# Unread products of two constant tiles in TensorE's waits: the last dense layer and the output stage of a graph network

## The chip, the cores and the metric

The kernel runs as one program on one core of a Trainium2 chip. The metric is device time in microseconds (us), from one launch, as the median of several runs. The engines are named as in the profile: PE is TensorE (PEld its weight loads), DVE is VectorE, ACT is ScalarE, POOL is GpSimd, SP is SyncE, which issues most DMAs here.

## The reference

The reference is a graph network of four blocks on 12,500 nodes with 128 features each and 212,500 edges sorted by destination. Each block normalizes x, computes a message-passing layer and adds its result to x:

```python
h = jnp.maximum(_layernorm(x, axis=-1), 0.0)
x = x + _L2_gnn_ref(h, edge_index, ...)      # ends with a batch norm and h @ fcW.T + fcb
h = jnp.maximum(_layernorm(x, axis=-1), 0.0)
x = x + _L3_gnn_ref(h, edge_attr_20, edge_weight, src, dst, ...)
# inside _L3_gnn_ref:
h = x @ W_in2f
Wij = ssp(f_ij @ W_filt1 + b_filt1) @ W_filt2 + b_filt2
Wij = Wij * rcut_ij[:, None]
x_ij = h[idx_j] * Wij
agg = jax.ops.segment_sum(x_ij, idx_i, num_segments=n_atoms)
out = ssp(agg @ W_out1 + b_out1) @ W_out2 + b_out2
```

`ssp` is the softplus less log 2. The first two blocks (relational layers with ten and three relations) and the third (two mean-aggregating layers) have the same form: a dense product per node, then a sum over edges.

## The kernel before, in words

Nodes are taken in 25 superblocks of 512 (four tiles of 128), edges in 104 groups of 16 tiles of 128. The kernel has seven edge passes, with dense stages (the list `DENSE`, k = 0 to 6) between them. A dense stage turns the sums of the pass before into the new x, normalizes it, and writes a table of products that the next pass gathers by edge. Stages 2, 3 and 4 ("flows") run mostly inside the pass that follows their data: `flow_keep` (L1741, all three stages) and `flow_init` (L1750, stages 3 and 4) are VectorE's parts of it, once for each of 25 superblocks. They stand between the one-hots and additions of the edge groups on VectorE's queue.

The change touches these functions, and the dense stages k = 5 and k = 6, which run by themselves, with no edge work beside them. Every engine has its own instruction stream; the order within one is the order in which the code is written, and engines meet at semaphores (`wait_ge`, `then_inc`).

**Stage 5, the last layer's dense work**, is a loop over superblocks with `body(f, l)` where f is one ahead of l. On TensorE a turn is: wait for y_ready; `update(f)` (L1561, L1562: for each of four tiles a product of one row of ones with the bias row fcb, then yT by fcw, into bank 0); wait for h; four transposes of h (L1592, bank 1); wait for hT; four products with the table's weights (L1604, banks 3 to 6). VectorE adds the update to xs (L2120), takes the layer norm's statistics (L2127 to L2137) and evacuates half of the table products (L2146). ScalarE makes, in this order, yT from the batch norm (L1179), hT (L1191), the square root (L1195), h (L1205) and the other half of the evacuations (L1213). SP stores x (L709) and loads the next xs (L705), POOL stores the table (L869).

**The filter pass**, the last edge pass, follows. Its `filter_product` opens with L1412, the product of `ones_b` (96 rows by 128, bf16) with `bfilt2_quad` (96 by 512, bf16), which spreads a bias over a bank. Both tiles are constant from the start of the kernel on.

**Stage 6, the output stage**, runs the same loop over superblocks in pairs. On TensorE a turn is: wait for the four partial sums of superblock f to be added (VectorE L2106, agg_step); four transposes (L1571, bank 1); wait for y_sum of the superblock before; `update(l)` with bout2 and wout2 (L1561, L1562); wait for y_copy and out_parts; one product of 512 columns, wout1 by the copied sums (L1580, bank 7). ScalarE copies the transposes (L1183) and makes the softplus in four steps (L929 to L934); VectorE adds the partial sums (L2106), the two softplus terms (L2111) and the update to xs (L2120). SP issues, in this order, four loads of partial sums for two superblocks ahead (L699), the load of xs (L705), and the store of x (L709); each is 256 KB.

PSUM banks 7 (in stage 5) and 5 (in stage 6) are not in use in their stages.

Of the kernel before, what the change touches and what calls it, by code (L numbers as in the profile page):

```python
# [68 lines left out]
def build(nc, d, out, n_nodes, n_edges):  # L69
# [9 lines left out]
    def turns(k, flag):  # L79

        return nsb * sum(bool(flag(p)) for j, p in enumerate(DENSE[:k]) if j and j not in FLOWS)
# [4 lines left out]
    def has_upd(p): return p["upd"] != ""  # L86
    def has_ln(p): return p["ln"]
    def has_root(p): return p["root"] != ""
    def has_table(p): return p["rels"] > 0
# [5 lines left out]
    def n_chunks(p):  # L95

        return 4 * len(cuts(p))
# [10 lines left out]
    def units(reps):  # L108

        return reps * in_pass + (nsb - in_pass)  # L110

    def stages_with(k, flag):

        return sum(bool(flag(DENSE[j])) for j in FLOWS if j < k)
# [19 lines left out]
    with ExitStack() as ctx:  # L134
        def sb(name, shape, dt=F32):
            return ctx.enter_context(nc.sbuf_tensor(name, shape, dt))

        def sem(name):
            return ctx.enter_context(nc.semaphore(name))
# [42 lines left out]
        bfilt2_quad = sb("bfilt2_quad", [3 * PART, BANK], BF16)  # L182
        bias_rest = sb("bias_rest", [1, P])
        part_b = sb("part_b", [1, P], BF16)
        ones_b = sb("ones_b", [3 * PART, P], BF16)
# [84 lines left out]
        ps = [ctx.enter_context(nc.psum_tensor(f"ps{k}", [P, BANK], F32)) for k in range(8)]  # L270
# [113 lines left out]
        s_keep = sem("s_keep")  # L384
        s_init = sem("s_init")
# [27 lines left out]
        def reps_of(e):  # L413

            e.wait_ge(reps_ready, 1)
            return e.value_load(reps_i[0:1, 0:1], min_val=1, max_val=nwin)

        def settle(e):

            e.sem_inc(settled, 1)  # L420

        def quads_before(reps, pn):

            return reps * (pn * 4 * ngroups)
# [41 lines left out]
        def tail(e, reps, body):  # L466

            with e.Fori(0, nsb - in_pass) as i:
                body(i + in_pass, e.snap(reps * in_pass + i))

        def so_far(reps, k, flag, t):

            return units(reps) * stages_with(k, flag) + t

        def chunks_so_far(reps, k, t):

            return units(reps) * flow_chunks(k) + t * n_chunks(DENSE[k])

        def all_chunks(reps, k):

            return units(reps) * flow_chunks(k + 1)
# [765 lines left out]
        def _(pe):  # L1247
# [13 lines left out]
            reps = reps_of(pe)  # L1261
# [204 lines left out]
            for c in range(n_attr):  # L1466
                n = min(P, ntiles - c * P)
                if c >= 4:
                    pe.wait_ge(typeT_ready, c - 3)
                pe.matmul(ps[c % 4][0:n, 0:P], etype[:, c * P:c * P + n], ident[:],  # L1470
                          start=True, stop=True).then_inc(typeT_mm, 1)
# [62 lines left out]
            for k, p in enumerate(DENSE):  # L1534
                if k == 0:
                    continue
                nck = n_chunks(p)
                hT = hT_s if has_ln(p) else yT
                pe.wait_ge(add_done, quads_before(reps, k + 1) + 4)
                settle(pe)  # L1540
                if k in FLOWS:
                    t = pe.snap(reps * in_pass)
                    pe.wait_ge(c_evac, chunks_so_far(reps, k, t) + 4)
                    if has_root(p):
                        pe.wait_ge(s_init, so_far(reps, k, has_root, t) + 1)
                    settle(pe)
                    tail(pe, reps, lambda f, t: flow_tail(k, f, t))
                    pe.wait_ge(c_evac, all_chunks(reps, k) + 4)
                    pe.wait_ge(s_init, units(reps) * stages_with(k + 1, has_root) + 1)
                    pe.wait_ge(s_x_new, units(reps) * stages_with(k + 1, has_x) + 1)  # L1550
                    settle(pe)
                    run_pass(k + 1)
                    continue

                def update(i):

                    pe.wait_ge(x_new, i + (turns(k, has_x) + 1))
                    for j in range(4):
                        o = ps[0][:, j * P:(j + 1) * P]
                        if "row" in p:  # L1560
                            pe.matmul(o, ones[0:1, :], bias_row[p["row"]][:], start=True, stop=False)  # L1561
                        mm = pe.matmul(o, yT[:, j * P:(j + 1) * P], W[p["upd"]][:], start="row" not in p, stop=True)  # L1562
                    mm.then_inc(upd_mm, 1)

                def body(f, l, b=0, uses=0):
                    if p["src"] == "sum":
                        if f is not None:
                            pe.wait_ge(agg_step, f * 3 + 3)
                            pe.wait_ge(y_copy, f + 1)
                            for j in range(4):  # L1570
                                mm = pe.matmul(ps[1][:, j * P:(j + 1) * P], agg_in[:, b, 0, j, :], ident[:],  # L1571
                                               start=True, stop=True)
                            mm.then_inc(aggT_mm, 1)
                        if l is not None:
                            pe.wait_ge(y_sum, l + 2)
                            update(l)
                        if f is not None:
                            pe.wait_ge(y_copy, f + 2)
                            pe.wait_ge(out_parts, f + 1)
                            pe.matmul(ps[7][:], W["wout1"][:], flat(h), start=True, stop=True).then_inc(out_mm, 1)  # L1580
                        return
                    if f is not None and has_upd(p):
                        pe.wait_ge(y_ready, f + (turns(k, has_src) + 1))
                        update(f)
                    if l is None:
                        return
                    if has_ln(p):
                        n = turns(k, has_ln)
                        pe.wait_ge(h_ready, l + (n + 1))
                        pe.wait_ge(hT_ready, l + (n + 1))  # L1590
                        for j in range(4):
                            mm = pe.matmul(ps[1][:, j * P:(j + 1) * P], h[:, j, :], ident[:], start=True, stop=True)  # L1592
                        mm.then_inc(hT_mm, 1)
                        pe.wait_ge(hT_ready, l + (n + 2))
                    elif has_table(p):
                        pe.wait_ge(y_ready, l + (turns(k, has_src) + 1))
                    if has_root(p):
                        pe.wait_ge(acc_init, l + (turns(k, has_root) + 1))
                        pe.matmul(ps[2][:], W[p["root"]][:], hT[:], start=True, stop=True).then_inc(root_mm, 1)
                    for c in range(nck):  # L1600
                        j, cut = c // len(cuts(p)), cuts(p)[c % len(cuts(p))]

                        pe.wait_ge((evac_a, evac_v)[c % 2], l * (nck // 2) + (chunks(k) // 2 + c // 2 + 1))
                        pe.matmul(ps[3 + c % 4][:, 0:cut[1] - cut[0]], hT[:, j * P:(j + 1) * P],  # L1604
                                  W[p["table"]][:, cut[0]:cut[1]], start=True, stop=True).then_inc(tab_mm, 1)

                superblocks(pe, p, body)
                if has_table(p):

                    pe.wait_ge(evac_a, 2 + chunks(k + 1) // 2)  # L1610
                    pe.wait_ge(evac_v, 2 + chunks(k + 1) // 2)
                    pe.wait_ge(acc_init, turns(k + 1, has_root) + 1)
                    pe.wait_ge(x_new, turns(k + 1, has_x) + 1)
                    run_pass(k + 1)
# [3 lines left out]
        def _(dve):  # L1618
# [62 lines left out]
            reps = reps_of(dve)  # L1681
# [53 lines left out]
            def flow_keep(k, f, t, adds):  # L1735

                acc_f = acc[:, bass.ds(f * SB, SB)]
                dve.wait_ge(add_done, adds)
                dve.wait_ge(s_y, so_far(reps, k, has_src, t) + 2)
                settle(dve)  # L1740
                dve.tensor_scalar(acc_f, acc_f, keep, bias_once, ALU.mult, ALU.add).then_inc(s_keep, 1)  # L1741

            def flow_init(k, f, t, bank, adds):

                acc_f = acc[:, bass.ds(f * SB, SB)]
                dve.wait_ge(add_done, adds)
                dve.wait_ge(s_root, so_far(reps, k, has_root, t) + 2)
                dve.wait_ge(s_keep, so_far(reps, k, has_src, t) + 2)
                settle(dve)
                dve.scalar_tensor_tensor(out=acc_f, in0=ps[bank][:], scalar=once, in1=acc_f, op0=ALU.mult, op1=ALU.add  # L1750
                                         ).then_inc(s_init, 1)

            def flow_x(k, t):

# [466 lines left out]
```

## Time and profile before

| what | value |
|---|---|
| median of three runs | 17679.55 us (17678.54 to 17693.12) |
| the profiled execution | 17666.72 us, its span 17665.0 us |
| mean granted TensorE clock | 0.623 |
| PE / PEld busy | 7873.9 us (45%) / 6273.0 us (36%) |
| DVE busy | 6843.6 us (39%) |
| ACT busy | 3221.2 us (18%) |
| POOL busy | 10730.4 us (61%) |
| mean DMA traffic | 81 GB/s |

The page is read from the top: busy time of each engine, then the course over 40 slices, then the chain of work that ended last. A granted clock of 1.0 is 2.4 GHz and one of 0.5 is 1.2 GHz; a number between them is a mean over a stretch in which both were granted. A share of busy time is a mean over stages with different limits, so the stages are read one at a time, by stretches of the span.

### The profile page before, as it was taken

What the parts mean: (1) busy time and instruction counts of PE and PEld (TensorE: products, weight loads), DVE (VectorE), ACT (ScalarE), POOL (GpSimd) and SP (SyncE); (2) the same over time, 40 slices, a digit from 0 to 9 for tenths busy, and PEclk for the clock granted to TensorE, in tenths of its full rate; (3) what the DMA queues carried; (4) which work ended last, traced back from release to release, by engine and by line L of the source; (5) the groups of instructions that cost most, each with busy time, mean ns of one, the idle gap of its engine ahead of it and who ended that gap; (6) DMA issues with size and microseconds to landing.
All of it is one profiled execution on the core that took longest, in us unless ns stands there. A gap on an engine that the chain in (4) does not pass through costs nothing.

```text
span 17665.0 us, 179568 instructions
## 1 busy us (share of the span) xinstructions
PE 7873.9 (45%) x36107; PEld 6273.0 (36%) x36108; DVE 6843.6 (39%) x28057; ACT 3221.2 (18%) x6961; POOL 10730.4 (61%) x10236
## 2 busy tenths in 40 slices
PE   5633333623333333333333333333333577777777
PEld 3333333322222223332332322222222455555555
DVE  8522222244444423323322222344544344444443
ACT  3422222300000000000000000000000144444443
POOL 0266666365555546666566666666666268888882
PEclk8755555856666555555555555555555577777775
DMA  2333333411111131111111111233333266666665
GB/s 102 125 88 89 89 88 88 175 47 53 54 54 53 53 104 53 52 52 51 51 46 46 47 47 47 60 87 85 87 86 87 66 113 118 117 117 118 117 118 122
DMA packets 1122539, 1438.17 MB, mean 81 GB/s; under 512 B 211981, under 2 KB 737444, under 8 KB 1122316
## 3 DMA queue, kind: packets, MB, share of 16 engines
q0 software_dynamic: 536912, 792.85, 21.0%
q1 hardware_dynamic: 531700, 613.30, 11.9%
q10 hardware_dynamic: 53748, 30.36, 0.6%
q14 instruction: 155, 1.27, 0.0%
q8 instruction: 24, 0.39, 0.0%
HBM read 1101.27 MB, written 334.40 MB: 81 GB/s over the span
## 4 chain that ended last, share of the span: by engine, by line
another core or an unknown queue 29%; issue 22%; DVE 21%; DMA 10%; POOL 6%; PE 5%; ACT 3%; DVEq 2%; ACTq 1%; SPq 0%; POOLq 0%
DMA agg_dram<-acc,sum_row 9%; DVE tab_s L1950 5%; POOL agg_dram L887 5%; DVE scratch L1950 4%; DVE xn_h L1958 3%; DVE scratch L1920 3%; DVE acc L1906 2%; DVE rows L1818 1%; PE ps L1604 1%; POOL scratch L901 1%; ACT hT_s L1009 1%; PE ps L1361 1%; PE ps L1561 1%; PE ps L1562 1%
## 5 line engine op out<-in xcount | busy, mean ns | idle before, releaser
L901 POOL DMA_INDIRECT scratch<-table_dram,row_st x4160 | 3966.4, 953 | 2541.5 <-ACT row_st L1040 1269.3
L901 POOL DMA_INDIRECT rows<-table_dram,row_st x4160 | 3964.0, 953 | 2321.5 <-issue 1247.3
L1361 PE MATMUL ps<-tab_s,rows 128*128 128x128 f32 x8320 | 1906.8, 390 | 3028.0 <-issue 1274.0
L1361 PE MATMUL ps<-scratch 128*128 128x128 f32 x8320 | 1829.5, 390 | 2873.1 <-DMA scratch<-table_dram,row_st 1247.8
L887 POOL DMA_INDIRECT agg_dram<-acc,sum_row x1664 | 2654.5, 1595 | 529.2 <-issue 391.2
L1361 PEld LDWEIGHTS ps<-tab_s,rows 128*128 128x128 f32 x8320 | 1694.4, 294 | 3214.8 <-issue 2149.0
L1361 PEld LDWEIGHTS ps<-scratch 128*128 128x128 f32 x8320 | 1617.8, 289 | 3058.3 <-issue 2119.2
L1906 DVE TENSOR_TENSOR acc<-ps,acc 128x128 f32 x2080 | 608.6, 293 | 4575.8 <-remote 4054.7
L1950 DVE TENSOR_SCALAR scratch<-ps,rw_st 128x128 f32<-128x128 f32 x3328 | 1114.3, 401 | 338.4 <-issue 227.4
L1920 DVE SCALAR_TENSOR_TENSOR scratch<-iota,rw_st,ps 128x128 f32<-128x128 f32 x2496 | 715.2, 343 | 1355.3 <-remote 873.9
L1950 DVE TENSOR_SCALAR tab_s<-ps,rw_st 128x128 f32<-128x128 f32 x3328 | 1112.2, 401 | 330.3 <-issue 247.0
L1271 PE MATMUL ps<-scratch,tab_s 128*128 128x128 f32 x3328 | 675.9, 367 | 808.0 <-DVE scratch L2041 774.6
L1040 ACT ACTIVATE row_st<-row_i 128x16 int32 (+1 forms) x520 | 109.3, 210 | 4819.1 <-remote 3200.6
L1271 PEld LDWEIGHTS ps<-scratch,tab_s 128*128 128x128 f32 x3328 | 595.9, 269 | 866.7 <-issue 866.1
L2035 DVE COPY sum_row<-etype 128x4 int32 x416 | 81.8, 197 | 1476.0 <-POOLq L886 1421.2
L1958 DVE SCALAR_TENSOR_TENSOR xn_h<-scratch,src_st,lower 128x128 f32<-128x128 int32 x1664 | 508.5, 347 | 346.8 <-issue 346.7
L1450 PE MATMUL ps<-scratch,acc 128*128 128x128 f32 x3328 | 601.1, 341 | 12.2 <-issue 7.3
L1450 PEld LDWEIGHTS ps<-scratch,acc 128*128 128x128 f32 x3328 | 566.0, 256 | 20.2 <-issue 20.1
L1406 PE MATMUL ps<-scratch,wfilt 20*128 20x512 f32 x836 | 557.5, 751 | 28.6 <-DMA scratch<-in_feat 22.3
L1414 PEld LDWEIGHTS ps<-wfilt,scratch 128*128 128x128 f32 x3336 | 516.7, 221 | 16.2
L1414 PE MATMUL ps<-wfilt,scratch 128*128 128x128 f32 x3336 | 513.6, 305 | 0.0
L946 ACT ACTIVATE yT<-acc 128x512 f32 (+1 forms) x75 | 47.2, 629 | 2352.9 <-DVE acc L1906 2330.7
(229 smaller groups left out, 10600.9 us busy)
## 6 DMA issues: line engine op xcount, KB each, us to landing
scratch<-in_src_row SPq DMA_DIRECT2D x832, 256.0 KB
table_dram<-tab_s POOLq DMA_DIRECT2D x200, 640.0 KB, 3.2
scratch<-type_dram SPq DMA_DIRECT2D x416, 256.0 KB
scratch<-in_dst_row SPq DMA_DIRECT2D x416, 256.0 KB
rows<-table_dram,row_st POOLq DMA_INDIRECT x4160
scratch<-table_dram,row_st POOLq DMA_INDIRECT x4160
scratch<-table_dram SPq DMA_DIRECT2D x416, 64.0 KB
agg_dram<-acc,sum_row POOLq DMA_INDIRECT x1664
```

What stands on the lines that cost most here:

```text
L887: pool.indirect_dma_start(agg_dram[j], bass.IndirectOffsetOnAxis(ap=sum_row[:, QUAD * q + j:QUAD * q + j + 1], axis=0), sums[:, q, j * P:( ...
L901: pool.indirect_dma_start(row_banks[bank][:, u, :], None, table_dram[k], bass.IndirectOffsetOnAxis(ap=row_st[:, bank, u:u + 1], axis=0)).t ...
L1009: act.activation(hT_s[:], type_row[:, q % 2, :], ACT.Abs, bias=rel_of[:, 3:4]).then_inc(relT_step, 1)
L1271: mm = pe.matmul(o, lhs[:, u, :], rhs[:, u, :], start=j == 0 or not summed, stop=j == QUAD - 1 or not summed)
L1361: mm = pe.matmul(ps[bank][:, q * P:(q + 1) * P], rows[:, u, :], hot[:, u, :], start=u % QUAD == 0, stop=u % QUAD == QUAD - 1)
L1406: pe.matmul(ps[4][:], wfilt1[:], feat[:, q, :], start=True, stop=True).then_inc(f1_mm, 1)
L1414: mm = pe.matmul(ps[6 + b][:, j * P:(j + 1) * P], f_buf[:, 2, b, j * P:(j + 1) * P], W["wfilt2"][:], start=False, stop=j == QUAD - 1)
L1450: mm = pe.matmul(ps[5][:, j * P:(j + 1) * P], hotT[:, q % 2, j * P:(j + 1) * P], nodes[:, q % 2, :], start=True, stop=True)
L1906: dve.tensor_tensor(window, ps[bank][:, q * P:(q + 1) * P], window, ALU.add).then_inc(add_done, 1)
L1920: i = dve.scalar_tensor_tensor(out=out(u), in0=iota[:], scalar=rw[:, 0, u:u + 1], in1=looked_up(j), op0=ALU.is_equal, op1=ALU.mult, accum_ ...
L1950: one_hots(q, lambda u: dve.tensor_scalar(hot[:, u, :], ps[7][:, 0:P], rw[:, 0, u:u + 1], rw[:, 1, u:u + 1], ALU.is_equal, ALU.mult))
L1958: i = dve.scalar_tensor_tensor(out=pairs[:, q % 2 * QUAD + j, :], in0=src_row[:, q, j * P:(j + 1) * P], scalar=src_st[:, bank, u:u + 1], i ...
```

## The change

TensorE gets a helper `fill(bank, times)` that multiplies the constant tiles `ones_b` and `bfilt2_quad` into a bank that nobody reads. In stage 5 it is called six times over ahead of the wait for y_ready, and three times over between the transposes and the wait for hT. In stage 6 it is called four times over at the start of a turn, and three times over ahead of the waits that precede L1580. Beside that, VectorE waits, behind each `flow_keep` and each `flow_init`, for the semaphore that this very instruction raises.

```diff
@@ -1562,8 +1562,14 @@
                     mm.then_inc(upd_mm, 1)
 
+                def fill(bank, times):
+
+                    for _ in range(times):
+                        pe.matmul(ps[bank][:], ones_b[:], bfilt2_quad[:], start=True, stop=True)
+
                 def body(f, l, b=0, uses=0):
                     if p["src"] == "sum":
+                        fill(5, 4)
                         if f is not None:
                             pe.wait_ge(agg_step, f * 3 + 3)
                             pe.wait_ge(y_copy, f + 1)
@@ -1575,11 +1581,13 @@
                             pe.wait_ge(y_sum, l + 2)
                             update(l)
                         if f is not None:
+                            fill(5, 3)
                             pe.wait_ge(y_copy, f + 2)
                             pe.wait_ge(out_parts, f + 1)
                             pe.matmul(ps[7][:], W["wout1"][:], flat(h), start=True, stop=True).then_inc(out_mm, 1)
                         return
                     if f is not None and has_upd(p):
+                        fill(7, 6)
                         pe.wait_ge(y_ready, f + (turns(k, has_src) + 1))
                         update(f)
                     if l is None:
@@ -1591,6 +1599,7 @@
                         mm.then_inc(hT_mm, 1)
+                        fill(7, 3)
                         pe.wait_ge(hT_ready, l + (n + 2))
@@ -1739,6 +1748,7 @@
                 dve.tensor_scalar(acc_f, acc_f, keep, bias_once, ALU.mult, ALU.add).then_inc(s_keep, 1)
+                dve.wait_ge(s_keep, so_far(reps, k, has_src, t) + 2)
@@ -1749,6 +1759,7 @@
                 dve.scalar_tensor_tensor(out=acc_f, in0=ps[bank][:], scalar=once, in1=acc_f, op0=ALU.mult, op1=ALU.add
                                          ).then_inc(s_init, 1)
+                dve.wait_ge(s_init, so_far(reps, k, has_root, t) + 2)
```

## Rows read from the trace of the kernel before

**Rows 1.** Busy time by stretch; the last three columns: clock, DMA share, GB/s

```profile
13892.00:14187.00 295.00, 238.93 (x792) 185.21 (x792) 75.53 (x348) 86.08 (x223) 18.14 (x24) 0.50 0.20 64
...
14210.00:17370.00 3160.00, 2302.57 (x11211) 1772.65 (x11209) 1391.74 (x4874) 1532.78 (x2494) 2651.10 (x1662) 0.77 0.68 117
...
17385.00:17665.00 280.00, 239.58 (x650) 154.42 (x650) 80.15 (x122) 77.40 (x125) 0.00 (x0) 0.51 0.46 133
```

**Rows 2.** Chain of waits by line: dense work, then output stage

```profile
by line: PE ps L1562 26.1%; PE ps L1561 25.0%; PE ps L1592 16.3%; issue 7.4%; PE ps L1604 6.4%; ACT yT L1179 5.7%; ACT hT_s L1191 4.8%; ACT xn_h L1205 3.9%; ACT tab_s L1213 3.1%; ACTq L506 0.6%; ACTq L566 0.4%; ACTq L1179 0.4%; ACTq L1190 0
...
by line: PE ps L1561 22.3%; PE ps L1562 21.7%; PE ps L1580 12.1%; issue 9.7%; DMA scratch<-agg_dram 7.5%; PE ps L1571 6.9%; DVE scratch L2106 5.9%; ACT hT_s L934 4.9%; DVE yT L2111 4.7%; ACT hT_s L932 4.2%; ACT tab_s L930 1.2%; ACT xn_h L11
```

**Rows 3.** Timeline, a turn of the dense work: start, us, engine, line, [idle]

```profile
14009.60 0.79 PE L1561 MATMUL ps<-fcb,ones 1*128 1x128 f32 x2 [1.25 <-ACT yT L1179]
...
14015.49 0.69 DVE L2120 TENSOR_TENSOR xn_h<-ps,xs 128x512 f32<-128x512 f32 x1 [6.82 <-PE ps L1562]
...
14018.00 2.07 PE L1604 MATMUL ps<-win,hT_s 128*128 128x128 f32 x8 [0.84 <-ACT hT_s L1191]
...
14018.51 1.65 ACT L1205 ACTIVATE xn_h<-xn_h,nrm 128x128 f32<-128x128 f32 x4 [0.45 <-DVE nrm L2137]
...
14021.32 0.79 PE L1561 MATMUL ps<-fcb,ones 1*128 1x128 f32 x2 [1.25 <-ACT yT L1179]
```

**Rows 4.** Timeline, one turn of the output stage

```profile
17507.88 0.69 DVE L2120 TENSOR_TENSOR xn_h<-ps,xs 128x512 f32<-128x512 f32 x1 [6.02 <-PE ps L1562]
...
17509.59 0.69 ACT L929 ACTIVATE hT_s<-ps,cols 128x512 f32<-128x512 f32 x1 [7.16 <-PE ps L1580]
...
17510.55 2.08 PE L1571 MATMUL ps<-ident,scratch 128*128 128x128 f32 x8 [1.00 <-DVE scratch L2106]
...
17511.63 0.37 SPq L705 DMA_DIRECT2D xs<-x_dram  x1
...
17512.98 0.79 PE L1561 MATMUL ps<-bout,ones 1*128 1x128 f32 x2 [0.35 <-DVE yT L2111]
...
17520.57 0.69 ACT L929 ACTIVATE hT_s<-ps,cols 128x512 f32<-128x512 f32 x1 [7.31 <-PE ps L1580]
```

**Rows 5.** DMA issues, output stage: count, KB each, us to landing

```profile
xs<-x_dram SPq DMA_DIRECT2D x23, 256.0 KB, 4.5
```

**Rows 6.** Timeline of TensorE in the filter pass, at half and at full clock

```profile
14262.16 0.61 PE L1412 MATMUL ps<-bfilt_quad,ones_b 96*128 96x512 bf16 x1
...
14262.56 1.91 PE L1414 MATMUL ps<-wfilt,scratch 128*128 128x128 f32 x8
...
14267.47 0.39 PE L1412 MATMUL ps<-bfilt_quad,ones_b 96*128 96x512 bf16 x1
...
14267.70 1.06 PE L1414 MATMUL ps<-wfilt,scratch 128*128 128x128 f32 x8
```

**Rows 7.** Timeline of TensorE at the start of the output stage

```profile
17389.67 1.91 PE L1571 MATMUL ps<-ident,scratch 128*128 128x128 f32 x8
...
17393.30 0.48 PE L1561 MATMUL ps<-bout,ones 1*128 1x128 f32 x2 [1.73 <-DVE yT L2111]
...
17393.71 0.49 PE L1562 MATMUL ps<-wout,yT 128*128 128x128 f32 x2
```

**Rows 8.** Busy time by microsecond there, columns as in rows 1

```profile
17391.00:17392.00 1.00, 0.57 (x3) 0.29 (x2) 0.00 (x0) 0.97 (x3) 0.00 (x0) 0.78 1.13 297
...
17394.00:17395.00 1.00, 1.00 (x6) 0.60 (x5) 0.00 (x0) 0.00 (x0) 0.00 (x0) 0.93 0.00 0
...
17395.00:17396.00 1.00, 1.00 (x4) 0.77 (x4) 0.00 (x0) 0.00 (x0) 0.00 (x0) 0.50 0.00 0
```

**Rows 9.** VectorE's wait on itself, and the two lines that get one

```profile
14017.23 0.38 DVE L2131 BATCH_NORM_AGGREGATE mv<-st 128x2 f32<-128x6 f32 x4 [0.15 <-DVE st L2127]
...
L1741 DVE TENSOR_SCALAR acc<-acc,final x75: 544/546/706, 3876.8 to 11319.8; - x72, 128x512 f32<-128x512 f32 x3
...
L1750 DVE SCALAR_TENSOR_TENSOR acc<-ps,final,acc x50: 749/751/753, 6675.6 to 11321.9; 128x512 f32 x48, 128x512 f32<-128x512 f32 x2
```

## The prediction, on record before the result was seen

> **What bounds the kernel now.** I read the table of stretches first [rows 1]. The change adds products to two stretches alone: the dense work of the last layer (13892 to 14187 us, 295 us) and the output stage (17385 to 17665 us, 280 us). The reader should see three things in those rows: together they are 575 us, 3% of the span; in both TensorE is busy for more than 80% of the time; and in both its granted clock is 0.50 or 0.51, the lower level (1.2 GHz), while the filter pass between them, where TensorE is busy for 73%, has 0.77, a mixture of both levels. So a busy share does not say which level is granted.
>
> The chain of waits says whose time this is [rows 2]. In the dense work TensorE's four lines hold some 74% of the chain, in the output stage 63%. TensorE sets the pace at half clock, so what the change can gain is TensorE's own time on the chain, and nothing else.
>
> Then I took one turn of each loop apart. **Dense work** [rows 3]: a turn is 11.72 us, from one L1561 (14009.60) to the next (14021.32). The update (eight products, alternating between one row of bias and 128 rows) lasts until VectorE starts at 14015.49, 5.89 us. VectorE and ScalarE then make the norm, 3.02 us to L1205, and h, the evacuation and the next yT take 2.81 us to the next L1561. The transposes (L1592) and the table products (L1604) run beside this; TensorE waits 0.84 us ahead of L1604 and 1.25 us ahead of L1561. **Output stage** [rows 4]: a turn is 10.98 us, from one L929 (17509.59) to the next. The softplus and VectorE's sum take 3.39 us to L1561, the update 5.8 us, the output product L1580 the other 1.8 us. TensorE waits 1.00 us ahead of L1571 and 0.35 us ahead of L1561.
>
> **The price of a fill.** The same product, ones_b by bfilt2_quad, stands in the filter pass as L1412 [rows 6]: from its start to that of the next is 0.40 us at half clock, 0.23 us at full clock. Twice 0.23 is 0.46, so I take 0.43 us and 0.22 us. There are 225 fills in the dense work (six and three a turn) and 179 in the output stage (four and three).
>
> **What full clock gives.** Eight 128-column halves take 1.91 us at half clock and 1.06 us at full clock [rows 6], so about 0.85 us less for four products. An update product is 0.41 us from start to start at full clock [rows 7], where the whole update at half clock is 5.8 us, 0.72 each: 3.3 us for eight, 2.5 us less.
>
> **A turn of the dense work with fills.** At full clock: 11.72 - 2.5 = 9.2 us. The fills hide: behind the update TensorE needs 0.9 (transposes), 0.8 (hT's copy with its hand-overs, with three fills of 0.66 inside), 0.9 (table products) and 1.3 us (six fills), 3.9 us, and yT comes 5.8 us after the update. At half clock they do not: 1.72 + 3 x 0.43 + 1.72 + 6 x 0.43 = 7.3 us behind an update of 5.8, 13.1 us, 1.4 us more than now. Queued behind the fills are the table products, whose evacuations have slack, and the next update, for which VectorE, ScalarE and everything else waits.
>
> **A turn of the output stage with fills.** The three fills in front of L1580 stand in no wait: L1580 follows the last update product with no idle time, so they lie on the chain whole, 0.66 us or 1.29 us. At full clock: 3.39 + 3.3 + 0.66 + 0.96 = 8.3 us. A second loop is then as long: the load of xs is issued 3.75 us after VectorE's L2120 (17507.88 to 17511.63) [rows 4], behind the store and four loads of sums on SP's queue, and lands 4.5 us later [rows 5], 8.25 us, and the next L2120 needs it. I take 8.4 us. At half clock: 10.98 + 1.29 = 12.3 us; four fills (1.7 us) in the wait of 1.00 us make L1571 late, but the output product, late itself, covers that.
>
> **Which clock.** The trace of before does not show these stages with fills; the ends are its two levels. Two places speak for a rise. At the start of the output stage L1571, on 128 rows, ran from 17389.67 to 17391.58 straight behind L1580, and the clock rose in the microsecond from 17391; the update began at 17393.30, and at the end of the microsecond from 17394 the clock fell back to 0.50, though TensorE was busy there without a gap [rows 7, 8]. Here the clock rose in products on 128 rows and fell in the update, half of whose products have one row. In the filter pass such blocks stand among waits of microseconds, and 0.77 is granted over its 3160 us [rows 1]. With fills, the 7.3 us between two updates become one closed block of products on 96 and 128 rows, so I expect a rise in nearly every turn and a fall in many updates: 0.8, that is 60% of the time at full clock. Output stage alike.
>
> Turns by rate: dense 0.6/9.2 + 0.4/13.1 gives 10.4 us, 1.3 less; output 0.6/8.4 + 0.4/12.3 gives 9.6 us, 1.36 less. Times 25: -32 and -34 us.
>
> The Trainium skill, page "TensorE: Matmul & The Clock Gate", section "Why this matters for your kernels", advises keeping TensorE busy without a break to get full clock and warns of idle gaps between bursts. This case's trace does not agree: 5.9 us of update without a gap, the transposes straight behind it, and no wait above 1.25 us [rows 3], at 0.50 [rows 1]. By that rule idle gaps are not what keeps the clock low here, closing them would buy nothing, and the sum would be that of the half-clock rival below.
>
> **The two new waits on VectorE.** After L1741 (75 times) and L1750 (50 times) VectorE waits for its own last result [rows 9]. No such wait stands there now; the nearest is VectorE's own wait between L2127 and L2131, 0.15 us [rows 9]. All 125 on the chain would be 19 us; none, 0. Behind them on VectorE stand the one-hots of the next group, which TensorE's gathered products need, but VectorE is busy for 39% of the span and POOL's gathers for 61% (the page's busy times), so nearly all is covered: 2 us. Nothing excludes a small gain from a different spacing, but no row suggests one.
>
> **Sum.** -32 - 34 + 2 = -64 us. The profiled execution took 17666.72 us (span 17665.0), 13 us under the median of the three runs, 17679.55; the sum gives 17603 for it and 17615 us for the median. A measurement of this kernel tells about 0.2%, 35 us, from no change.
>
> **Rivals.**
> *The clock stays at half.* The fills do not count for what raises it, or each update takes it away at once. Then 25 x 1.4 + 25 x 1.3 + 2 = 69 us more, 17749: slower. Place: in front of L1561 in the dense work, in front of L1580 in the output stage. It decides from a granted clock below about 0.63, where both stages break even (dense: 28% of the time at full clock; output: 26%). For it: 80% busy and 0.50 now [rows 1]. Against: the rise at 17391 [rows 8]. Chance 0.06.
> *The change does less than it says:* the clock flips, at 0.65 (30%), and fills at half clock eat the gain: 11.6 and 10.8 us a turn, 5 us less in all, about 17675. For it: the fall in mid-update [rows 8]. Chance 0.11.
> *Full clock throughout:* 25 x 2.5 + 25 x 2.6 - 2 = 125 us less, 17554. For it: no long waits remain. Against: again the fall in the update. The loads of xs bound the output stage in this case. Chance 0.08.
> *The forecast*, granted clock 0.7 to 0.9: 0.75. At 0.7 the turns are 11.2 and 10.4 us, 26 us less in all; at 0.9, 9.8 and 9.0 us, 96 us less. That is 17583 to 17653. Some 8 us for the spread of runs at the lower end; at the upper one I reach into the second rival and the full 19 us of waits: 17575 to 17665. Left out are half clock, full clock and half of the second rival, 0.19.
> Faster by over 0.2% is a granted clock above 0.71: nearly all of the forecast and the full-clock case, 0.82. Within 0.2%: the rest of the forecast and the second rival, 0.12. Slower: 0.06.
>
> **What would show it.** Granted clock 0.7 to 0.9 in both stages, with L1561's products now at 0.41 and now at 0.72 us; the stage's turns at 10.4 and 9.6 us; no idle time in front of the table products at half clock; waits of L2120 for xs in turns at full clock; the passes between 3540 and 13870 unchanged within a few us, and the filter pass too. I am wrong if the clock in either stage is below 0.63, if it is full throughout, or if the difference of the spans lies outside these two stages.

## The result, and the profile after

The changed kernel took 17622.51 us (median of 6 runs, 17601.45 to 17637.92) beside 17681.67 us for the kernel before on the same chip (17665.79 to 17702.44): ratio 0.9965, interval 0.9955 to 0.9976. The profiled execution took 17604.58 us, its span 17602.8. The helper stands at L1568 now; L1571, L1580, L2106, L2111 and L2120 of before are L1577, L1587, L2117, L2122 and L2131, and L1592 and L1604 are L1600 and L1613; VectorE's L1741 and L1750 are L1750 and L1760.

Busy time by stretch of the changed kernel, columns as in [rows 1]:

```profile
13896.00:14143.00 247.00, 218.24 (x1019) 150.57 (x1019) 74.48 (x348) 86.15 (x223) 18.13 (x24) 0.83 0.24 78
14160.00:17320.00 3160.00, 2299.78 (x11244) 1773.39 (x11243) 1406.99 (x4885) 1537.01 (x2501) 2646.59 (x1659) 0.78 0.67 117
17340.00:17600.00 260.00, 229.51 (x825) 137.16 (x825) 80.61 (x124) 75.83 (x125) 0.00 (x0) 0.74 0.50 144
```

The granted clock (third number from the end) went from 0.50 to 0.83 in the dense work and from 0.51 to 0.74 in the output stage; the filter pass stayed where it was (0.77 before, 0.78 after). The stage starts and turns give the difference of the spans. They are read from the start of each update's first product by yT (L1562), and each sum is over the 24 turns between 25 superblocks:

| kernel | span | dense work starts | 24 dense turns (mean) | filter pass | 24 output turns (mean) |
|---|---|---|---|---|---|
| before | 17665.0 | 13893.3 | 281.1 (11.71) | 3219.3 | 262.7 (10.95) |
| after | 17602.8 | 13897.2 | 233.5 (9.73) | 3219.2 | 244.5 (10.19) |
| difference | -62.2 | +3.9 | -47.6 | -0.1 | -18.2 |

So the time came from the two stages, three quarters of it from the dense work. There, a turn at full clock and one with a fall of the clock in it, TensorE's timeline (start, us, engine, line, idle time before it):

```profile
14025.00 0.48 PE L1561 MATMUL ps<-fcb,ones 1*128 1x128 f32 x2 [0.48 <-ACT yT L1179]
...
14028.23 1.06 PE L1600 MATMUL ps<-ident,xn_h 128*128 128x128 f32 x8
...
14034.26 0.48 PE L1561 MATMUL ps<-fcb,ones 1*128 1x128 f32 x2 [1.68 <-ACT yT L1179]
...
14036.98 0.79 PE L1561 MATMUL ps<-fcb,ones 1*128 1x128 f32 x2
14037.70 0.80 PE L1562 MATMUL ps<-fcw,yT 128*128 128x128 f32 x2
14038.28 1.91 PE L1600 MATMUL ps<-ident,xn_h 128*128 128x128 f32 x8
14039.99 1.49 PE L1568 MATMUL ps<-bfilt_quad,ones_b 96*128 96x512 bf16 x3
14041.27 1.92 PE L1613 MATMUL ps<-win,hT_s 128*128 128x128 f32 x8
14042.98 1.61 PE L1568 MATMUL ps<-bfilt_quad,ones_b 96*128 96x512 bf16 x6
14044.51 0.48 PE L1561 MATMUL ps<-fcb,ones 1*128 1x128 f32 x2
14044.93 0.49 PE L1562 MATMUL ps<-fcw,yT 128*128 128x128 f32 x2
```

From 14025.00 to 14034.26 is 9.26 us, a turn wholly at full clock. In the next one the clock falls in the update (the last products take 0.72 us from start to start, 14036.98 to 14037.70), and has risen again before the next one (0.42 us from 14044.51 to 14044.93, and the six fills take 1.53 us where half clock would take 2.6). That turn is 10.25 us long. Its update takes 4.02 us to L1600 instead of 3.23, and the block behind it 6.23 us to the next L1561 instead of 6.03: although its transposes, first fills and table products ran at half clock, the 1.68 us that TensorE otherwise waits in front of L1561 swallowed nearly all of that. The 24 turns of the stage bear this out: fourteen take 9.25 or 9.26 us, although in three of them the clock is at half for a third of the time; two take 9.37 and 9.56, and six, with half clock for two thirds of the time, 10.23 to 10.50 us. The first two (11.49 and 11.41 us) come before and around the first rise.

Two turns of the output stage, TensorE's timeline:

```profile
17482.59 0.48 PE L1561 MATMUL ps<-bout,ones 1*128 1x128 f32 x2 [0.96 <-DVE yT L2122]
...
17484.52 0.79 PE L1561 MATMUL ps<-bout,ones 1*128 1x128 f32 x2
...
17487.28 1.49 PE L1568 MATMUL ps<-bfilt_quad,ones_b 96*128 96x512 bf16 x3
17488.56 1.92 PE L1587 MATMUL ps<-xn_h,wout 128*128 128x512 f32 x2
17490.27 1.26 PE L1568 MATMUL ps<-bfilt_quad,ones_b 96*128 96x512 bf16 x4
17491.36 1.06 PE L1577 MATMUL ps<-ident,scratch 128*128 128x128 f32 x8
17493.90 0.48 PE L1561 MATMUL ps<-bout,ones 1*128 1x128 f32 x2 [1.48 <-DVE yT L2122]
...
17497.13 1.06 PE L1568 MATMUL ps<-bfilt_quad,ones_b 96*128 96x512 bf16 x3
17497.99 1.91 PE L1587 MATMUL ps<-xn_h,wout 128*128 128x512 f32 x2
```

The first turn is 11.31 us (17482.59 to 17493.90), longer than one of before. The clock fell in the update, and the three fills (1.28 us) and L1587 (1.71 us) then ran at half clock, with no wait in front of them: everything behind L1587, the softplus first, was that much later. The rise comes with the fills of the next turn, too late for both. The second update is at full clock to its end and the fall comes in the fills behind it (three in 0.86 us instead of 0.66). Microseconds of the same stretch, columns as above, put the fall at the end of the one from 17483 and the rise in the one from 17490:

```profile
17483.00:17484.00 1.00, 1.00 (x6) 0.76 (x6) 0.00 (x0) 0.00 (x0) 0.00 (x0) 0.95 0.61 181
17484.00:17485.00 1.00, 1.00 (x4) 0.78 (x4) 0.00 (x0) 0.00 (x0) 0.00 (x0) 0.50 0.00 0
...
17490.00:17491.00 1.00, 1.00 (x4) 0.34 (x3) 0.14 (x1) 0.49 (x1) 0.00 (x0) 0.64 0.39 111
17491.00:17492.00 1.00, 1.00 (x9) 0.86 (x8) 0.00 (x0) 1.00 (x3) 0.00 (x0) 1.00 1.11 332
```

The chain of waits of the output stage, here from 17480 to 17540, now has the fills in it:

```profile
by line: PE ps L1562 21.3%; PE ps L1561 20.6%; PE ps L1587 14.3%; PE ps L1568 11.5%; issue 9.9%; ACT hT_s L934 7.3%; DVE yT L2122 7.0%; ACT hT_s L932 6.4%; ACT tab_s L930 1.4%; ACT hT_s L929 0.8%
```

The new waits on VectorE, outside both stages, first before and then after (VectorE's timeline):

```profile
7728.93 0.75 DVE L1750 SCALAR_TENSOR_TENSOR acc<-ps,final,acc 128x512 f32 x1 [0.27 <-issue]
7729.65 2.01 DVE L1950 TENSOR_SCALAR tab_s<-ps,rw_st 128x128 f32<-128x128 f32 x6
```

```profile
7729.32 0.75 DVE L1760 SCALAR_TENSOR_TENSOR acc<-ps,final,acc 128x512 f32 x1 [0.27 <-issue]
7730.80 1.05 DVE L1961 TENSOR_SCALAR tab_s<-ps,rw_st 128x128 f32<-128x128 f32 x3 [0.73 <-DVE acc L1760]
```

Where the next instruction followed at once, VectorE is idle for 0.73 us. Over the kernel the lines that follow L1760 wait 36.8 us for it in 38 places, but that counts idle time that stood there before too. Between the 50 instructions of this line and the ones behind them VectorE is idle for 58.2 us, where it was 41.2: 27 places had no gap before, and now 31 have one of 0.73 to 0.75 us, while most of the others had one of 1.3 us or more anyway. Behind flow_keep (L1750 now) it is 111.2 us instead of 103.5, with some 0.32 us in 20 places, where 19 had no gap before. So some 25 us of idle time are new. The start of the dense work, behind all of them, moved by 3.9 us.

### The profile page after: what moved, and what is told of

It is laid out like the page before. It is cut to its first block, busy times and chain, and to the rows that moved or that the text cites. A ratio compares the mean times of both kernels' runs of the same rounds, so it can differ in the third digit from the quotient of the medians.

```text
span 17602.8 us, 180416 instructions
## 1 busy us (share of the span) xinstructions
PE 7840.7 (45%) x36511; PEld 6225.4 (35%) x36512; DVE 6855.7 (39%) x28057; ACT 3219.7 (18%) x6961; POOL 10739.4 (61%) x10236
## 4 chain that ended last, share of the span: by engine, by line
another core or an unknown queue 30%; DVE 22%; issue 22%; DMA 10%; POOL 5%; PE 5%; ACT 3%; DVEq 2%; ACTq 1%; POOLq 0%; SPq 0%
DMA agg_dram<-acc,sum_row 9%; DVE tab_s L1961 5%; DVE scratch L1961 5%; POOL agg_dram L887 4%; DVE xn_h L1969 3%; DVE scratch L1931 3%; DVE acc L1917 2%; DVE rows L1829 1%; PE ps L1613 1%; ACT hT_s L1009 1%; DVEq L428 1%; PE ps L1361 1%; ACT xn_h L1012 1%; PE ps L1562 1%
## 5 line engine op out<-in xcount | busy, mean ns | idle before, releaser
L848 POOL DMA_DIRECT2D table_dram<-tab_s x100 | 53.9, 539 | 686.8 <-ACT tab_s L1098 686.8
```

## The experiments

Each kernel was run beside the kernel before on one chip, in three groups: e1 to e4 (before: 17847.07 us), e5 to e8 (17854.68 us) and e9 to e11 (15568.44 us). These chips differ by up to 2.3 ms in the passes ahead of the dense work, and the times of one kernel on the first two vary by up to 130 us, so I compare ratios on one chip, and the sums of 24 turns, which the kernel before's stages and e3's (a kernel that changes neither) give alike on different chips. The code excerpts show the difference to the changed kernel in e1 to e5 and e11, to the kernel before in e6 and e7, and otherwise to the run that is named; they are shortened, and the helper `fill` is left out of them.

**e1: the dense work's fills alone.**

```diff
-                        fill(5, 4)
-                            fill(5, 3)
-                dve.wait_ge(s_keep, ...)
-                dve.wait_ge(s_init, ...)
```

> The change's fills in the dense work alone (six and three a turn); no fills in the output stage, no new waits on VectorE. Reading of the trace after: the dense work is about 49 us shorter than before and the output stage as before (10.99 us a turn). So the span should be 49 us under that of before (about 17616), granted clock 0.8 or more in the dense work, 0.50 in the output stage. Rival (the gain is split as the prediction had it, 32 and 34 us): 32 us less.

Measured: ratio 0.9972 (0.9949 to 0.9994). Dense turns 236.4 us in all at a clock of 0.80, output turns 263.6 us at 0.50. The dense fills alone bring 45 us of turns, the part that the whole change got there, and touch nothing else.

**e2: the output stage's fills alone.**

```diff
-                        fill(7, 6)
-                        fill(7, 3)
-                dve.wait_ge(s_keep, ...)
-                dve.wait_ge(s_init, ...)
```

> The change's fills in the output stage alone (four and three a turn); dense work and VectorE as before. Reading of the trace after: some 17 us less in the output stage, turns alternating between about 9.3 and 11.3 us, granted clock near 0.74; dense work 11.72 us a turn. Rival (as predicted): 34 us less, turns of 9.6 us on average.

Measured: ratio 1.0005 (0.9984 to 1.0025), which tells nothing of 20 us. Output turns 241.8 us at 0.77, dense turns 281.2 us at 0.50: 21 us of turns. The split into some -47 and some -20 is therefore not a matter of one trace.

**e3: the two waits on VectorE alone.** All four calls of `fill` are taken out.

> The two new waits on VectorE alone, no fills. The prediction took 2 us, with 0 and 19 us as ends; the dense work of the changed kernel begins 3.9 us later than before. If the waits are hidden, the span is within 5 us of that of before and the difference between the starts of the dense work is noise; if they lie on the chain, the passes before the dense work take up to 19 us more.

Measured: ratio 1.0013 (0.9996 to 1.0031), turns 281.1 and 262.4 us, both at 0.50. Its dense work started at 14029.1, earlier than that of e1, e2 and e4 (14050.3 to 14114.9), of which only e4 has the waits as well. A cost of 19 us would be a ratio of 1.0011, which lies close to the middle of the interval, and no cost at all lies in it too. The run doesn't decide between them.

**e4: all fills, with one row instead of 96.** The same instructions, columns and places; only the number of rows that are multiplied differs.

```diff
-                        pe.matmul(ps[bank][:], ones_b[:], bfilt2_quad[:], start=True, stop=True)
+                        pe.matmul(ps[bank][:], ones_b[0:1, :], bfilt2_quad[0:1, :], start=True, stop=True)
```

> The changed kernel with every fill cut to one row: ones_b[0:1] by bfilt2_quad[0:1], the same count of instructions and columns, so the same time on TensorE. If what matters is that TensorE is not idle, this kernel has the clock and the time of the changed kernel (62 us less than before). If products on few rows do not bring the clock up, it stays at 0.50 in both stages, and the fills only cost: dense turns of 13.1 us, output turns of 12.3 us, 68 us more than before or somewhat over that, since each change between one row and 128 rows costs about 0.3 us.

Measured: ratio 1.0068 (1.005 to 1.0086), the slowest of all. Its stages, dense work and output stage, columns as in [rows 1]:

```profile
14115.00:14432.00 317.00, 314.02 (x967) 203.52 (x967) 72.56 (x334) 84.75 (x213) 17.42 (x23) 0.50 0.18 59
17657.00:17969.00 312.00, 310.46 (x787) 165.49 (x786) 76.75 (x117) 74.11 (x120) 0.00 (x0) 0.50 0.40 114
```

TensorE is busy for 99% of both stretches, and its granted clock is 0.50 from end to end. Closing the gaps isn't what raised the clock in the changed kernel; products on many rows are. How many rows between one and 96 it takes was not tried. Only three of the 96 rows of `bfilt2_quad` hold anything but zeros, so the fills that raised the clock multiplied mostly zeros. The run is at the same time the half-clock rival of the prediction, made real: dense turns 13.19 us (priced at 13.1), output turns 12.98 us (priced at 12.3).

**e5: seven fills at the start of the output turn, none in front of the output product.** As many as in the change, all where TensorE waits.

```diff
-                        fill(5, 4)
+                        fill(5, 7)
-                            fill(5, 3)
```

> The changed kernel with the three fills ahead of L1580 moved to the start of the output stage's turn: seven there, none between the update and the output product. Theory: the three fills stood on the chain (0.66 us at full clock, 1.29 us at half clock) and the seven now stand in the wait for the sums, in one block with L1580 and L1571. The output stage's turn should fall from 10.2 us to about 8.6 us (40 us less over the stage), near the 8.3 us at which the loads of xs would bound it, granted clock 0.8 or more. Rival: the place of the fills does not matter, 10.2 us a turn as in the changed kernel. Dense work as in the changed kernel (9.7 to 9.9 us a turn).

Measured: ratio 0.9941 (0.9922 to 0.9961). Output turns 210.9 us at 0.86, 34 us less than the change's; dense turns 234.8 us, as after. VectorE's waits in this stage, here from 17490 to 17700, have a new row:

```profile
DVE xn_h L2130 <- DMA xs<-x_dram: 47.9, 10, 6.0
```

So in 10 of these turns (14 of the stage's 25, 67.2 us) VectorE's addition waited last for the load of xs, as the prediction had it for full clock. The changed kernel has no such wait: all 25 of its L2131 waited for L1562.

**e6: no fills and no waits; the four bias products of an update become one of 512 columns.**

```diff
+                        pe.matmul(ps[0][:, :].rearrange("p (j c) -> p j c", j=4), ones[0:1, :],
+                                  bias_row[p["row"]][:, :].unsqueeze(1).broadcast_to([1, 4, P]), start=True, stop=False)
...
-                            pe.matmul(o, ones[0:1, :], bias_row[p["row"]][:], start=True, stop=False)
```

> The kernel before, no fills, with the update's products regrouped: one bias product of one row by 512 columns first, then the four of yT, so that TensorE changes between one row and 128 rows twice instead of eight times. Theory: each change costs about 0.3 us at half clock, so the update falls from 5.8 us to about 4.0 us and the turns to about 9.9 us (dense) and 9.1 us (output), more than the fills gave, with the clock mostly at 0.50 to 0.6. Rival (the 0.72 us of an update product are its own time, not the changes): turns as before, 11.72 and 10.98 us.

Measured: ratio 0.9932 (0.9907 to 0.9957). Dense turns 238.4 us and output turns 218.2 us, both at a clock of only 0.59. TensorE's timeline of an update at half clock:

```profile
14204.76 2.07 PE L1559 MATMUL ps<-fcb,ones 1*128 1x512 f32 x2 [2.17 <-ACT yT L1179]
14206.75 2.08 PE L1562 MATMUL ps<-fcw,yT 128*128 128x128 f32 x8
14208.62 1.92 PE L1598 MATMUL ps<-ident,xn_h 128*128 128x128 f32 x8
```

The same columns take 3.86 us from the first product to the transposes. Before, they took 5.64, from 14009.60 [rows 3] to

```profile
14015.24 1.92 PE L1592 MATMUL ps<-ident,xn_h 128*128 128x128 f32 x8
```

There eight products alternated between one and 128 rows, seven changes; now there is one, so each change between row counts cost about 1.78 / 6 = 0.3 us at half clock. That there are fewer products now explains little: the four by yT, each with its own weights, take 1.87 us in a row, 0.47 each, where every product of the alternating update took 0.72.

**e7: as e6, with the bias product in the form of the fill** (bf16, 96 rows, 512 columns, from a tile built once at the start).

```diff
+                        pe.matmul(ps[0][:], ones_b[:], quad_of[p["row"]][:], start=True, stop=False)
```

> The kernel before, no fills, with the update's bias made by one bf16 product of 96 rows by 512 columns, as L1412 makes it in the filter pass (fcb and bout2 split in three bf16 parts, in two new constant tiles). Theory: the update becomes dense, 0.43 us and four products, about 2.2 us at half clock and 1.1 us at full clock; without a fill the clock then rises by itself in part of the turns (0.65 to 0.7), dense turns of about 8 us, output turns of 8.3 us where the loads of xs bound them. Some 8 us more in the setup for the new tiles. Rival: without fills the clock stays at 0.50: dense turns of 9.2 us or so, output turns of about 8.4 us.

Measured: ratio 0.9912 (0.9879 to 0.9944). Dense turns 196.2 us at 0.62, output turns 202.3 us at 0.74, without one unread product.

**e8: e7 with nine fills in the dense turn and seven at the start of the output turn.**

```diff
+                        fill(5, 7)
+                        fill(7, 6)
+                        fill(7, 3)
```

> The update of e7 with fills: six and three a turn in the dense work, seven at the start of the turn in the output stage. Theory: the clock is full nearly throughout (0.95), dense turns of 7.0 to 7.3 us, output turns of 8.3 us as in e7. So over e7 the fills buy about 20 us in the dense work and nothing in the output stage. Rival (fills lengthen the now shorter turns): no less than e7.

Measured: ratio 0.9912 (0.9884 to 0.9941), no different from e7's. Dense turns 174.0 us at 0.94, output turns 198.5 us at 0.91. In the dense work the fills still bring 22 us; TensorE's timeline of a turn there:

```profile
14199.83 0.39 PE L1560 MATMUL ps<-fcb_quad,ones_b 96*128 96x512 bf16 x1 [1.68 <-ACT yT L1180]
14200.06 1.05 PE L1562 MATMUL ps<-fcw,yT 128*128 128x128 f32 x8
14200.95 1.06 PE L1600 MATMUL ps<-ident,xn_h 128*128 128x128 f32 x8
...
14206.99 0.39 PE L1560 MATMUL ps<-fcb_quad,ones_b 96*128 96x512 bf16 x1 [1.68 <-ACT yT L1180]
```

The update takes 1.12 us to L1600, where the changed kernel's takes 3.23, and the turn 7.16 us. In the output stage the higher clock brings 4 us of turns, because another loop is the bound; its waits, its chain and its DMA issues:

```profile
DVE xn_h L2130 <- DMA xs<-x_dram: 105.8, 20, 6.0
```

```profile
by line: DMA xs<-x_dram 52.8%; SPq L700 22.8%; issue 8.9%; DVE xn_h L2130 7.8%; SPq L710 4.7%; SPq L706 0.9%; SPq L719 0.8%; DVEq L2125 0.4%; DVEq L2129 0.4%; SPq L421 0.2%; SPq L705 0.2%; SPq L697 0.2%
```

```profile
xs<-x_dram SPq DMA_DIRECT2D x21, 256.0 KB, 4.5
```

Load of xs, the queue of loads of sums ahead of it (L700) and L2130: the loop of the prediction's output part.

**e9: e8, and SP issues the load of xs ahead of the four loads of sums.**

```diff
-                                    load_sums(i * 2 + (b + 2), b)
-                                    move_x(i * 2 + b)
+                                    move_x(i * 2 + b, lambda: load_sums(i * 2 + (b + 2), b))
```

> e8 with the load of xs moved ahead of the four loads of sums on SP's queue in the output stage. Theory: in e7 and e8 the output stage is bound by the loop from VectorE's sum into xn over SP's queue (store, four loads, load of xs) back to the next sum, 8.3 us a turn; with the load of xs first the engines' own loop is left, 5.6 to 6.5 us a turn, some 45 to 60 us less than e8; dense work as in e8 (7.2 us). Rival: the bytes themselves are the bound (1.5 MB a turn), and the turn stays above 8 us.

Measured: ratio 0.9869 (0.9852 to 0.9885), the best. Output turns 166.2 us (6.93 each), 32 us less than e8's; dense turns 174.6 us. The loads of sums are the next bound; waits, chain of waits and stages (columns as in [rows 1]):

```profile
DVE scratch L2114 <- DMA scratch<-agg_dram: 53.5, 15, 33.5
```

```profile
by line: DMA scratch<-agg_dram 34.1%; PE ps L1560 12.1%; SPq L700 10.3%; PE ps L1576 10.1%; issue 9.6%; DVE scratch L2114 9.5%; DVE xn_h L2128 5.0%; SPq L706 3.2%; SPq L711 2.8%; PE ps L1558 2.8%; PE ps L1585 1.2%; ACT hT_s L933 0.5%; DVE y
```

```profile
11796.00:11971.00 175.00, 132.61 (x802) 92.88 (x801) 70.53 (x334) 82.55 (x213) 17.39 (x23) 0.94 0.33 105
...
15187.00:15353.00 166.00, 128.88 (x617) 82.42 (x616) 77.06 (x117) 74.26 (x120) 0.00 (x0) 0.89 0.74 215
```

Of the 53.5 us of waiting, 33.5 are one wait ahead of the stage's first turn, so the other 14 waits sum to 20 us. The load of xs gains twice: it is no longer issued behind the four loads of sums, and it lands sooner, in 2.9 us where e8 has 4.5, while the loads of sums take 4.1 us instead of 3.8:

```profile
xs<-x_dram SPq DMA_DIRECT2D x24, 256.0 KB, 2.9
```

e8 was traced on another chip, but the store of x takes 2.2 us on both.

**e10: e9 without the fills**, so e7 with SP's new order.

> e9 without any fill (e7 with the load of xs first). Tells whether fills still buy something once TensorE's update is dense and the loads of xs are out of the way. Theory: output turns of 6.3 to 6.6 us with the clock at 0.8 or so (e9: 5.6 to 6.0), dense work as in e7, 8.2 us. Rival (the rest is not TensorE's): same output turn as e9.

Measured: ratio 0.9889 (0.9872 to 0.9905); dense turns 191.1 us at 0.68, output turns 175.2 us at 0.75. The two medians differ by 28.7 us, the turns by 16.5 + 9.0 = 25.5 us: that is what unread products are worth once the update is regrouped.

**e11: e5 with SP's new order**, the update as before.

> e5 (the changed kernel, seven fills at the start of the output stage's turn) with the load of xs first, the update as in the kernel before. Theory: the turn falls from 8.8 to about 8.2 us; few turns wait for xs. Rival: unchanged, 8.8 us.

Measured: ratio 0.9926 (0.9909 to 0.9942); dense turns 234.8 us at 0.82, output turns 193.7 us at 0.91, where e5 has 210.9. Without this wait the alternating update sets the turn (its two lines hold 41% of the chain of waits): 8.07 us beside 6.93 in e9.

## Why the prediction was right, and where its terms were not

**The sum was right by luck, its split was not.** Forecast: -32 dense, -34 output, +2 for the waits, -64 in all, 17603 us for the profiled execution. Measured: -47.6, -18.2, +3.9 at the start of the dense work, -62.2 us of span. Two errors of 16 us cancelled, and e1 and e2 (-45 and -21 us of turns) repeat both.

**The clock lay in the range**: 0.83 and 0.74, inside the 0.7 to 0.9 forecast (0.8 was taken for both), falling in the update as [rows 8] showed it at the stage's start. The table products at half clock had no idle time in front of them, and the filter pass stayed, as forecast; the turns, forecast at 10.4 and 9.6 us, came out at 9.73 and 10.19. What raises it was named by row count, and e4 bears that out: 99% busy, with the fills on one row, 0.50. The page "TensorE: Matmul & The Clock Gate" of the Trainium skill (section "Why this matters for your kernels") advises keeping TensorE busy without a break and leaving no long idle gaps between bursts. e4 disagrees with the first part: no gaps, and 0.50. No run tests the second part by itself: e7 is idle for up to 4.4 us in a turn of the output stage and has 0.74 there, where the kernel before, never idle for more than some 1.3 us in a dense turn, has 0.50; but e7's clock falls too, in nearly every turn, and its gaps may be why.

**The step that failed in the dense work** is "turns by rate: 0.6/9.2 + 0.4/13.1". Both ends were right: 9.26 us at full clock, 13.19 at half (e4). But apart from the first, which has no transposes or table products yet, no turn is at half clock whole. The clock fell late in the update and rose again in the fills ahead of the next, so that the half-clock time lay mostly in the block beside VectorE's and ScalarE's work, of which 1.68 us was waiting. A turn with a fall cost 1.0 us more, not 3.9. The share of full clock explains less: at the measured 0.83 the same formula gives 10.24 us, not 9.73. Rate-weighting two ends holds only if the slow level falls evenly over the chain. A reading behind the ends was off as well, by little: the update takes 5.64 us to the next product in both stages, not 5.8, and what follows it in the output turn 1.95 us, not 1.8.

**The step that failed in the output stage** is "Output stage alike": 0.8, 60% of the time at full clock, taken over from the dense work. The stage got 0.74, some 48%, and with that the same formula, 0.48/8.4 + 0.52/12.3, gives 10.06 us, near the 10.19 measured. So most of the 0.6 us by which a turn exceeds its forecast is the share of full clock, and only the rest the price of its ends. With the ends that the traces show, 8.33 us for the one turn wholly at full clock and 12.98 for e4's at half, it would be 10.24. Where the fall comes tells the single turns apart: about the same share of full clock (0.34 to 0.40) makes turns of 10.3 and of 11.4 us. In the longer ones, as from 17482.59, the fall comes early in the update, and the update, the three fills and the output product run slow with nothing to cover them. In the shorter ones, as from 17419.78, it comes at the update's end, and the last of the slow time lies in the four fills and the transposes of the next turn, which partly run in TensorE's wait. Of e5's 34 us over the change, 16 to 31 us are what three fills on the chain cost (24 turns at 0.66 or 1.29 us; 1.28 measured at half clock), as I had priced them; beside that the clock rose to 0.86. Why the three fills in front of the output product went with a lower share isn't taken apart.

**The loop of xs** was rightly priced as a mean (8.25 us; e8's turns, bound by it, take 8.27), and wrongly taken for a floor of each turn: single turns of e5 are as short as 7.6 us and of e8 5.5 us, made up by longer ones. In the changed kernel it never showed, since the clock's falls kept the turns above it; I had expected some such waits.

**The waits on VectorE** cost 0.73 us behind L1760 and 0.32 us behind L1750 where the next instruction used to follow at once, not 0.15, the row I had read [rows 9]. The new idle time is some 25 us, more than my upper bound of 19 for all. Nearly all of it was covered, as forecast, though no run shows that POOL's gathers are what covered it: 3.9 us at the start of the dense work, within what two executions differ by anyway, and no loss that e3 could show.

**The rivals.** Full clock throughout didn't come about in any run. With the update regrouped, e8 and e9 come near (0.89 to 0.94), but so does the output stage of e11 (0.91), which keeps the alternating update. The second rival, fills that eat the gain, is what the output stage did in its longest turns. Half clock was excluded by the granted clock of both stages, and e4 shows that it would have been +84 us of turns, where the price was some 67; the 0.7 us by which each output turn exceeds its price isn't taken apart. Its fills there bring four more changes of row count a turn, which e6 prices at up to 0.3 us each.

## What to carry to other kernels

When TensorE is at half clock although it is busy, look at the rows of its products before its gaps: here the kernel stood at 0.50 while 81% busy, and at 99% with more one-row products. Mending the product itself (one bias product of 512 columns on 96 rows ahead of four others) was worth 85 us in the dense turns and 60 in the output turns (e7), more than all unread products, which are better put where the engine waits than in front of a product that the chain needs (e5). When mixing a fast and a slow state into a mean, estimate the share of each for every stage by itself and ask at which instruction the state changes; and behind each gain look for the loop that comes next: TensorE, then the load of xs, then the loads of sums.

## What the runs showed of the hardware that I had not expected

- A change of the row count between neighbouring products costs about 0.3 us at half clock: 5.64 us for the alternating update, 3.86 us for the same columns grouped (e6).
- A TensorE that is busy for 99% of 317 us stayed at 0.50 when its extra products had one row (e4).
- VectorE's wait for its own last result cost 0.73 to 0.75 us behind one 128x512 operation (L1760) and 0.32 us behind another (L1750), and 0.15 us between the short statistics instructions [rows 9].
- The load of xs landed in 4.5 us when it was issued behind four loads of sums (e8) and in 2.9 us when it was issued ahead of them (e9).
- The same kernel took 17681.67, 17847.07, 17854.68 and 15568.44 us in the four measurements, each on one chip. The dense work starts at 13897.2 us in the changed kernel on the first and at 11796.0 us in e9 on the last, while the filter pass takes 3219.2 and 3216.3 us; POOL's busy time is the same (10739.4 and 10748.8 us), so what differs is waiting in the passes before. Its cause wasn't looked for.
